# An RWKV layer with a routed mixture of experts on one core: other opening and closing steps, and expert slots spread over three more places

## The chip, the cores and the metric

The kernel runs on one core of one Trainium2 chip, as one program. The metric is the device time of one execution in microseconds. Before the change it is 512.9 us, the median of three runs (509.98, 512.90, 513.15). The profile is of one further execution.

## What is computed

8192 tokens (32 sequences of 256) of 128 channels, all in float32. Each token is normalised, goes through an RWKV block (time mixing with the WKV recurrence, then channel mixing) and, beside it, through a mixture of 8 experts (one shared expert for all, one routed expert for each token). The two results are multiplied, and the input is added:

```python
xn = _layernorm(x)
# s: the RWKV block of xn
h = _ln(xn); hx = _shift(h)
k, v, sr = (h*tmk + hx*(1-tmk)) @ att_kw.T, (h*tmv + hx*(1-tmv)) @ att_vw.T, sigmoid((h*tmr + hx*(1-tmr)) @ att_rw.T)
x2 = xn + (sr * _wkv(time_decay, time_first, k, v)) @ att_ow.T
h = _ln(x2); hx = _shift(h)
kk = square(relu((h*f_tmk + hx*(1-f_tmk)) @ f_kw.T))
s = x2 + sigmoid((h*f_tmr + hx*(1-f_tmr)) @ f_rw.T) * (kk @ f_vw.T)
# m: shared expert plus the one routed expert of the largest logit, both silu(x@wg.T)*(x@wu.T)@wd.T
m = swiglu(xn, shared) + swiglu(xn * sigmoid(max logit), expert[argmax logit])
out = x + silu(m) * s
```

## The kernel before, in words

**Tiling.** A tile is 128 tokens, a chunk is 512 tokens (two sequences, four tiles); there are 16 chunks, c = 0 to 15. PENULT is chunk 14 and LAST chunk 15. Every engine has its own program, written out by hand; semaphores tie them together. TensorE (PE) does matmuls and transposes, VectorE (DVE) scans and sums, ScalarE (ACT) activations and copies out of PSUM, GpSimd (POOL) small statistics, some 128x512 operations and the DMAs that it issues itself, SyncE (SP) all other DMAs.

**Opening.** For each chunk: x is loaded (L277), DVE takes statistics (`first_stats`, L1056) and combines them (`first_aggregate`, L1062), which it does for chunk c-1 after the statistics of chunk c. POOL makes the inverse deviation and the bias (L905 to L911), ACT normalises (`first_xn`, L625), PE transposes (L339) and ACT copies to the tile XT (`first_xt`, L631). Logits for the routing and the first parts of the shared expert are interleaved. Weights are loaded from ACT's queue (L619), eight DMAs before ACT's first activation. POOL's `second_rstd` (L915 to L921) gives what `make_z1` (L1129) needs.

**Steps.** From step i = 1 to 14 (`step(i)` of each engine) the WKV of chunk i, the channel mixing of chunk i-1 and its end for chunk i-2 run side by side. Eight places k = 0 to 7 in a step hold fill-in work, given by the table PLAN: parts of the shared expert and the routing in steps 1 to 5, then the expert slots. An expert slot n does, for one of 71 tiles of 128 sorted tokens, eight matmuls up (L473), two matmuls down of slot n-2 (L487), one transpose (L480), on ACT two or three activations (L737, L745, L728), on DVE one product (L1249) and on POOL a scatter of the rows to DRAM (L961). Slots 71 and 72 only finish those before them. Up to step 5, POOL also scatters the tokens to DRAM in expert order (L953). In the middle of all this SP copies x of chunks 0 to 11 to the output by one DMA from DRAM to DRAM (L300), once the first expert weights are on their way.

In each step ACT switches its table twice (L800 to the exp and log set, L810 back), and the work between is a chain through ACT and DVE.

**Closing** (`last_steps`). Chunks 14 and 15 finish. For both, x2 is made by DVE (L1199, with L1202 and L1206), its inverse deviation by POOL (`rstd_of_x2`, L935 to L941), z2 by ACT (L680), transposed by PE (`z2_transpose`, L398), turned to h2 (L689), mixed by DVE (`channel_mixes`, L1213 and L1216), and goes through the matmuls `ffn_receptance` (L405), `ffn_key` (L420) and `ffn_value` (L430). Meanwhile routed and shared output are added for all 16 chunks, in two ways: the odd chunks are loaded by SP (L313) into four buffers RR and added on PE by two matmuls with the identity (`final_sum`, L499 and L500); the even ones are added to XT by a DMA of POOL that accumulates (`final_add`, L975). ACT applies silu (L754, L758), DVE multiplies (`final_gate`, L1255). For chunks 0 to 11 a DMA of POOL adds the result to the copy of x in the output (`final_store`, L983); for chunks 12 to 15 DVE adds x (L1259) and SP stores (L317).

Of the kernel before, what the change touches and what calls it, by code (L numbers as in the profile page):

```python
# [7 lines left out]
P = 128  # L8
CHUNK = 512
# [23 lines left out]
NCST = K_TOK + TILES  # L33
# [3 lines left out]
ADDED = 12  # L37


def plan():  # L40
# [26 lines left out]
BY_PE = list(range(1, CHUNKS, 2))  # L67
BY_DMA = list(range(0, CHUNKS, 2))


def program(nc, x, vecs, cst, att_w, f_kw, f_vw, gate_w, sh_up, sh_dn, ex_w, out):
# [7 lines left out]
    with ctx:  # L79
# [71 lines left out]
        RR = [EW[u][:, 0:CHUNK] for u in range(4)]  # L151
# [8 lines left out]
        s_wa = sem("attention_and_shared_weights_loaded")  # L160
        s_fill = sem("xs_dram_filled")
# [41 lines left out]
        s_fx = [sem(f"final_x_loaded{u}") for u in range(4)]  # L203
        s_fr_in = [sem(f"final_routed_loaded{u}") for u in range(4)]
        s_fa = [sem(f"final_routed_added{u}") for u in range(4)]
        s_fy, s_fw, s_fv, s_fo = sem("final_y"), sem("final_silu"), sem("final_gated"), sem("final_out")
        s_pre, s_last = sem("x_copied_to_out"), sem("last_chunks_stored")
        s_out = [sem(f"out_stored{u}") for u in range(4)]
# [38 lines left out]

        RT_CHOSEN = 4
# [24 lines left out]
        def _(sp):  # L273
# [5 lines left out]
            for c in range(CHUNKS):  # L279
                load_x(c)  # L280
            sp.wait_ge(s_pad, 2)
# [18 lines left out]
            sp.dma_start(out[0:ADDED * CHUNK, :], x[0:ADDED * CHUNK, :]).then_inc(s_pre, 16)  # L300
            for c in range(5):
                sp.wait_ge(s_sct[c], 16 * TPC * (1 if c < 4 else CHUNKS - 4))
            for n in range(NEW + AHEAD):
                load_rows(n)
            for n in range(NEW, XTILES):
                load_weights(n)
                if n + AHEAD < XTILES:
                    load_rows(n + AHEAD)

            def load_final_routed(n):  # L310
                if n >= 4:
                    sp.wait_ge(s_fy, n - 3)
                sp.dma_start(tiles(RR[n % 4]), rows(routed_dram, BY_PE[n])).then_inc(s_fr_in[n % 4], 16)  # L313

            def store(c):
                sp.wait_ge(s_fo, c - ADDED + 1)
                sp.dma_start(rows(out, c), xn(c)).then_inc(s_last, 16)  # L317

            sp.wait_ge(s_xn, CHUNKS)
            for c in range(ADDED, CHUNKS):  # L320
                sp.dma_start(tiles(XI[c % 4][:, :]), rows(x, c)).then_inc(s_fx[c % 4], 16)
            for u in range(NXH):
                sp.wait_ge(s_yo[u], 16 * sum(1 for m in range(2, XTILES + 2) if m % NXH == u))
            for n in range(len(BY_PE)):
                load_final_routed(n)
            for c in range(ADDED, CHUNKS):
                store(c)
            for u in range(4):
                sp.wait_ge(s_out[u], 16 * (ADDED // 4))
            sp.wait_ge(s_last, 16 * (CHUNKS - ADDED))  # L330

        @block.tensor
        def _(pe):
# [67 lines left out]
            def ffn_receptance(c):  # L401
                pe.wait_ge(s_mix2, 2 * c + 1)
                b = BK if c == LAST else FB
                for j in range(TPC):
                    last = nc.tensor.matmul(part(b, j, CH), part(XR2, j, P), part(ATT, 4, CH), start=True, stop=True)  # L405
                last.then_inc(s_fr, 1)

            def ffn_key(c, q):
                if q == 0:
                    pe.wait_ge(s_mix2, 2 * c + 2)  # L410
# [3 lines left out]
                elif q == 1 and c == LAST:  # L414
                    pe.wait_ge(s_rk, 4 * c)
                elif q == 1:
# [3 lines left out]
                nc.tensor.matmul((FA, FB)[q % 2][:, :], part(FKW, q, P), XK2[:, :], start=True, stop=True)\  # L420
# [70 lines left out]
            def final_sum(n):  # L491
                b, c = RING[n % 3], BY_PE[n]
                pe.wait_ge(s_fr_in[n % 4], 16 * (n // 4 + 1))
# [5 lines left out]
                nc.tensor.matmul(b[:, :], ident, RR[n % 4], start=True, stop=False)  # L499
# [933 lines left out]
```

## Time and profile before

| what | value |
|---|---|
| median of the runs | 512.9 us |
| the profiled execution | 512.97 us |
| its span, first to last instruction | 511.2 us |
| busy: PE, DVE, ACT, POOL | 87%, 78%, 69%, 60% |

The span is 1.8 us shorter than the execution's own time, and all times below count from its start. An engine's busy time says how long its instructions ran, not whether anything waited for them; that is read from the timeline, where a row has its start, its length, the engine and line, what it writes and reads, and in brackets the idle time before it with what ended it.

### The profile page before, as it was taken

The numbers are of one execution on the slowest core, as the hardware profiler recorded it, in microseconds if no ns is written. First come the engines' busy times: TensorE is split into PE (matmuls) and PEld (weight loads), VectorE is DVE, ScalarE is ACT, GpSimd is POOL, SyncE is SP. The second block draws the span as 40 slices with busy tenths as digits, with TensorE's granted clock in tenths as the row PEclk, the third lists the DMA queues.
The fourth block names the chain that finished last, engine by engine and source line by source line (L and its number), as shares of the span: only waits on it lengthen the run. The fifth ranks groups of instructions, "written<-read, shape, count | busy, mean of one in ns | idle before, by whom it ended". The sixth has DMA issues, their size and how long they took to land. (4 is left out here: it accounts for less than half of the span.)

```text
span 511.2 us, 8965 instructions
## 1 busy us (share of the span) xinstructions
PE 446.2 (87%) x2655; PEld 332.9 (65%) x2655; DVE 397.5 (78%) x788; ACT 350.6 (69%) x706; POOL 307.5 (60%) x339
## 2 busy tenths in 40 slices
PE   0899897789899899899999999999999999977990
PEld 0567675356366465769696969686969696844650
DVE  4473959979669695979797979797979796987672
ACT  3768767375373746788787877778887887684860
POOL 6843686288677787228383838372828282846871
PEclk9999998599899999999999999999999999997996
DMA  8792000012911101226565556454656554427799
GB/s 270 224 275 60 2 0 1 5 48 88 378 50 48 44 32 49 54 79 168 164 167 163 173 157 177 153 160 131 173 159 177 155 171 147 124 82 121 107 189 161
DMA packets 62592, 64.97 MB, mean 127 GB/s; under 512 B 5776, under 2 KB 50705, under 8 KB 62496
## 3 DMA queue, kind: packets, MB, share of 16 engines
q1 hardware_dynamic: 46512, 49.06, 34.1%
q0 software_dynamic: 14880, 13.78, 13.0%
q10 hardware_dynamic: 1152, 1.56, 0.9%
q8 instruction: 22, 0.36, 0.3%
q14 instruction: 26, 0.21, 0.1%
HBM read 46.86 MB, written 21.12 MB: 133 GB/s over the span
## 5 line engine op out<-in xcount | busy, mean ns | idle before, releaser
L961 POOL DMA_INDIRECT routed_out<-xh,xs x71 | 94.1, 1326 | 46.5 <-ACT xh L745 30.0
L953 POOL DMA_INDIRECT tokens_by_expert<-xn,pos x64 | 66.8, 1044 | 27.8 <-issue 27.8
L473 PEld LDWEIGHTS bank_ring<-xh,ew 128*128 128x128 f32 x568 | 70.3, 192 | 10.6 <-issue 9.6
L473 PE MATMUL bank_ring<-xh,ew 128*128 128x128 f32 x568 | 75.4, 276 | 1.3 <-DVE hx L1249 0.8
L430 PE MATMUL bank_out<-fvw,kk 128*128 128x128 f32 x512 | 66.0, 275 | 0.0
L1224 DVE TENSOR_TENSOR kk<-rk 128x512 f32<-128x512 f32 x32 | 22.7, 711 | 53.3 <-ACT rk L703 49.8
L430 PEld LDWEIGHTS bank_out<-fvw,kk 128*128 128x128 f32 x512 | 61.9, 192 | 2.9 <-issue 2.9
L737 ACT ACTIVATE px<-bank_ring 128x256 f32<-128x256 f32 x71 | 27.0, 380 | 26.0 <-PE bank_ring L473 21.5
L487 PE MATMUL bank_ring<-ew,hx 128*128 128x128 f32 x284 | 43.5, 276 | 0.4 <-issue 0.4
L935 POOL TENSOR_SCALAR x_sm<-x_mv 128x4 f32<-128x4 f32 x16 | 4.4, 274 | 61.5 <-DVE x_mv L1206 60.7
L1241 DVE TENSOR_TENSOR hs<-tg,bank_ring 128x512 f32<-128x512 f32 x32 | 21.6, 676 | 24.6 <-ACT tg L721 11.0
L487 PEld LDWEIGHTS bank_ring<-ew,hx 128*128 128x128 f32 x284 | 37.8, 193 | 0.6 <-issue 0.6
L440 PEld LDWEIGHTS bank_ring<-sdn,hs 128*128 128x128 f32 x256 | 30.7, 192 | 11.3 <-DVE hs L1241 6.4
L451 PE MATMUL bank_ring<-xt,sup 128*128 128x512 f32 x64 | 35.9, 644 | 1.6 <-issue 1.6
L420 PE MATMUL bank_fb<-xk,fkw 128*128 128x512 f32 x64 | 33.7, 609 | 3.2 <-ACT tf L697 2.4
L457 PE MATMUL bank_ring<-xt,sup 128*128 128x512 f32 x64 | 35.5, 638 | 0.5 <-issue 0.3
L949 POOL TENSOR_TENSOR rw<-den_num,lq 128x512 f32<-128x512 f32 x16 | 22.2, 1387 | 21.5 <-issue 19.6
L745 ACT ACTIVATE xh<-bank_ring 128x256 f32<-128x256 f32 (+1 forms) x75 | 27.8, 370 | 8.2 <-PE bank_ring L487 5.6
L680 ACT ACTIVATE z<-x,x_sm 128x128 f32<-128x128 f32 x64 | 26.4, 483 | 10.2 <-POOL x_sm L941 10.2
L440 PE MATMUL bank_ring<-sdn,hs 128*128 128x128 f32 x256 | 31.6, 276 | 2.1 <-DVE hs L1241 2.1
L420 PE MATMUL bank_fa<-xk,fkw 128*128 128x512 f32 x64 | 32.9, 596 | 0.0
L1249 DVE TENSOR_TENSOR hx<-px,bank_ring 128x256 f32<-128x256 f32 x71 | 29.1, 409 | 0.5 <-ACT px L737 0.5
(167 smaller groups left out, 1116.8 us busy)
## 6 DMA issues: line engine op xcount, KB each, us to landing
ew<-ex_w SPq DMA_DIRECT2D x71, 384.0 KB
tokens_by_expert<-pad_row SPq DMA_DIRECT2D x1, 4686.0 KB, 21.4
xs<-tokens_by_expert SPq DMA_DIRECT2D x71, 66.0 KB
xi<-x SPq DMA_DIRECT2D x12, 256.0 KB, 4.5
out<-xn POOLq DMA_DIRECT2D x12, 256.0 KB, 8.2
ew<-routed_out SPq DMA_DIRECT2D x8, 256.0 KB, 4.2
xt<-routed_out POOLq DMA_DIRECT2D x8, 256.0 KB, 6.3
routed_out<-xh,xs POOLq DMA_INDIRECT x71
```

Source lines behind the costliest of these rows:

```text
L420: nc.tensor.matmul((FA, FB)[q % 2][:, :], part(FKW, q, P), XK2[:, :], start=True, stop=True)\
L430: last = nc.tensor.matmul(part(BO, j, CH), KK[:, q * CHUNK + j * P:q * CHUNK + (j + 1) * P], part(FVW, q, CH), start=(q + j == 0), stop=(q ...
L440: last = nc.tensor.matmul(part(b, j, CH), h[:, q * CHUNK + j * P:q * CHUNK + (j + 1) * P], part(SDN, q, CH), start=(q == 0), stop=(q == EQ ...
L451: nc.tensor.matmul(ring(5 * m + 3 * q)[:, :], part(SUP, q, P), part(XT, m, CHUNK), start=True, stop=True)\
L457: nc.tensor.matmul(ring(5 * m + 3 * q + 1)[:, :], part(SUP, EQ + q, P), part(XT, m, CHUNK), start=True, stop=True).then_inc(s_su, 1)
L473: last = nc.tensor.matmul(part(GU[n % 2], q, P), part(w, q, P), xt[:, 0:P], start=True, stop=True)
L487: last = nc.tensor.matmul(BX[:, P:P + CH], part(h, q, P), part(w, 2 * EQ + q, CH), start=(q == 0), stop=(q == EQ - 1))
L737: nc.scalar.activation(PX[n % 2][:, :], GU[n % 2][:, 0:EF], ACT.Silu).then_inc(s_px, 1)
L745: nc.scalar.activation(XH[n % NXH][:, a:b], BX[:, a:b], ACT.Copy).then_inc(s_xh, 1)
L953: nc.gpsimd.indirect_dma_start(xs_dram, bass.IndirectOffsetOnAxis(ap=POS[:, t:t + 1], axis=0), XN[:, t * XROW:(t + 1) * XROW], None).then_ ...
L961: nc.gpsimd.indirect_dma_start(routed_dram, bass.IndirectOffsetOnAxis(ap=XS[(n - 2) % NXS][:, CH:CH + 1].bitcast(i32), axis=0), XH[n % NXH ...
L1249: nc.vector.tensor_tensor(HX[n % NHX][:, :], PX[n % 2][:, :], GU[n % 2][:, EF:2 * EF], ALU.mult)\
```

## The change

1. **Opening.** DVE combines the statistics of chunks 0 to 3 right after taking them. ACT loads its second table only after the third chunk. `token_numbers` of POOL moves from behind the first chunk to behind chunk 3. The two channel-mixing weights (FKW, FVW) are loaded by SP after x of chunk 11, not by ACT at the start.
2. **No copy of x to the output.** Instead x of chunks 0 to 9 is loaded by SP between the loads of the expert slots (one after every fifth) into ten buffers, chunks 10 to 15 when a buffer is free again.
3. **Expert slots** are spread over 78 places in place of 75: places 0 to 2 of the last step are added.
4. **Closing.** POOL issues no DMAs any more. SP loads the routed output of all 16 chunks into ten buffers. Nine chunks are added by POOL with a 128x512 addition, seven on PE. x is added by POOL for chunks 0 to 14, by DVE for 15, and SP stores all chunks. The inverse deviation of x2 for chunks 14 and 15 is made by ACT (`Ln`, then `Exp`), the bias still by POOL. The product rw of chunk 15 moves from POOL to DVE. x2 of chunk 14 moves behind the WKV of chunk 15. The mixes of chunk 15 have tiles of their own (E1, E2), and the order of the last step is another on each engine.

```diff
     places = [(E_STEP, k) for k in range(5, 8)] + [(i, k) for i in range(E_STEP + 1, CHUNKS - 1) for k in range(8)]
+    places += [(CHUNKS - 1, k) for k in range(3)]
...
-BY_PE = list(range(1, CHUNKS, 2))
-BY_DMA = list(range(0, CHUNKS, 2))
+BY_PE = [1, 3, 5, 7, 9, 11, 13]
+BY_POOL = [c for c in range(CHUNKS) if c not in BY_PE]
+NRR, NXB = 10, 10
...
-            sp.dma_start(out[0:ADDED * CHUNK, :], x[0:ADDED * CHUNK, :]).then_inc(s_pre, 16)
...
+            def load_final_x(c):
...
+                elif c >= NXB:
+                    sp.wait_ge(s_fo, c - NXB + 1)
+                sp.dma_start(tiles(XB[c % NXB]), rows(x, c)).then_inc(s_fx0 if c < NXB else s_fx[c - NXB], 16)
...
+                if n % 5 == 0 and 3 <= n // 5 < 3 + NXB:
+                    load_final_x(n // 5 - 3)
...
+            for c in range(CHUNKS):
+                load_final_routed(c)
+            for c in range(CHUNKS):
                 store(c)
+                if c + NXB < CHUNKS:
+                    load_final_x(c + NXB)
...
@@ scalar
-            nc.scalar.preload_act_table_set("silu_and_others")
             for c in range(CHUNKS):
                 first_xn(c)
+                if c == 2:
+                    nc.scalar.preload_act_table_set("silu_and_others")
...
+            def rstd_of_x2(c):
+                act.wait_ge(s_mv2, TPC * (c + 1))
...
+                nc.scalar.activation(SM2[:, 0:TPC], stats(MV2, 0, TPC)[1], ACT.Ln, bias=CST[:, K_EPS:K_EPS + 1])\
+                  .then_inc(s_sm2, 1)
...
+                nc.scalar.activation(SM2[:, TPC:2 * TPC], SM2[:, 0:TPC], ACT.Exp, scale=-0.5).then_inc(s_rs2, 1)
...
                 nc.scalar.preload_act_table_set("natural_log_exp_and_others")
+                inverse_of_den(LAST)
+                rstd_of_x2(PENULT)
                 make_z2(PENULT)
-                inverse_of_den(LAST)
                 make_h2(PENULT)
+                rstd_of_x2(LAST)
+                make_z2(LAST)
                 nc.scalar.preload_act_table_set("silu_and_others")
+                make_h2(LAST)
...
@@ gpsimd
+            def final_sum(n):
+                c = BY_POOL[n]
+                y = part(XT, c, CHUNK)
...
+                nc.gpsimd.tensor_tensor(y, RR[c % NRR], y, ALU.add).then_inc(s_fp, 1)
+
+            def final_out(c):
                 pool.wait_ge(s_fv, c + 1)
...
+                nc.gpsimd.tensor_tensor(xn(c), xn(c), tiles(XB[c % NXB]), ALU.add).then_inc(s_fo, 1)
...
@@ vector
+            def make_rw(c):
...
+                nc.vector.tensor_tensor(RW[:, :], NUM, LQ[:, :], ALU.mult).then_inc(s_rw, 1)
...
                 first_stats(c)
-                if c > 0:
+                if c < 4:
+                    first_aggregate(c)
+                elif c > 4:
                     first_aggregate(c - 1)
```

The order of work at the places that matter most. DVE at the very start of the opening, before the change (bs holds partial statistics, mv the combined ones):

```order
L1056 BN_STATS bs<-xi 128x6 x8
L1062 BN_AGGR mv<-bs 128x2 x4
L1354 TENSOR_SCALAR vectors<-vectors 128x1
L1056 BN_STATS bs<-xi 128x6 x4
L1062 BN_AGGR mv<-bs 128x2 x4
```

and with the change:

```order
L1126 BN_STATS bs<-xi 128x6 x4
L1132 BN_AGGR mv<-bs 128x2 x4
L1126 BN_STATS bs<-xi 128x6 x4
L1132 BN_AGGR mv<-bs 128x2 x4
L1445 TENSOR_SCALAR vectors<-vectors 128x1
```

The first chunk's statistics are now combined before those of the second are taken.

DVE in the last step, from the mixes of chunk 14 on, before the change (x_1 is x2 of chunk 15, d and then xr, xk the mixes, kk the squares, xn<-xt,xn the final products):

```order
L1213 TENSOR_TENSOR d<-h 128x512
L1216 SCALAR_TENSOR_TENSOR xr<-d,vectors,h 128x512
L1216 SCALAR_TENSOR_TENSOR xk<-d,vectors,h 128x512
L1199 TENSOR_TENSOR x_1<-bank_k,xn 128x512
L1202 BN_STATS x_bs<-x_1 128x6 x4
L1206 BN_AGGR x_mv<-x_bs 128x2 x4
L1224 TENSOR_TENSOR kk<-rk 128x512 x2
L1255 TENSOR_TENSOR xn<-xt,xn 128x4x128 x2
L1213 TENSOR_TENSOR d<-h 128x512
L1216 SCALAR_TENSOR_TENSOR xr<-d,vectors,h 128x512
L1216 SCALAR_TENSOR_TENSOR xk<-d,vectors,h 128x512
```

and with the change:

```order
L1269 TENSOR_TENSOR x_1<-bank_k,xn 128x512
L1272 BN_STATS x_bs<-x_1 128x6 x4
L1276 BN_AGGR x_mv<-x_bs 128x2 x4
L1287 TENSOR_TENSOR d<-h 128x512
L1290 SCALAR_TENSOR_TENSOR xr<-d,vectors,h 128x512
L1290 SCALAR_TENSOR_TENSOR xk<-d,vectors,h 128x512
L1298 TENSOR_TENSOR kk<-rk 128x512
L1287 TENSOR_TENSOR d<-h 128x512
L1290 SCALAR_TENSOR_TENSOR e<-d,vectors,h 128x512 x2
L1298 TENSOR_TENSOR kk<-rk 128x512
L1329 TENSOR_TENSOR xn<-xt,xn 128x4x128 x2
```

The mixes of chunk 14 now stand behind x2 of chunk 15, and the mixes of chunk 15 between the two squares of chunk 14.

POOL in the last step, before the change (xt holds shared plus routed output, xn the product, x_sm the small statistics of x2):

```order
L975 DMA xt<-routed_out 128x4x128 x3
L949 TENSOR_TENSOR rw<-den_num,lq 128x512
L975 DMA xt<-routed_out 128x4x128
L935 TENSOR_SCALAR x_sm<-x_mv 128x4
L936 TENSOR_SCALAR x_sm<-x_mv 128x4
L938 TENSOR_TENSOR x_sm<-x_sm,minus_half 128x4
L941 TENSOR_TENSOR x_sm<-x_sm 128x4
L975 DMA xt<-routed_out 128x4x128 x4
L983 DMA out<-xn 128x4x128 x12
```

and with the change, up to the first of the additions of x (ew, d, xv and z are buffers of the routed output):

```order
L1005 DMA routed_out<-xh,xs 8192x128 x2
L1026 TENSOR_TENSOR xt<-ew,xt 128x512 x2
L1014 TENSOR_SCALAR x_sm<-x_mv 128x4
L1018 TENSOR_TENSOR x_sm<-x_sm 128x4
L1026 TENSOR_TENSOR xt<-ew,xt 128x512
L1014 TENSOR_SCALAR x_sm<-x_mv 128x4
L1018 TENSOR_TENSOR x_sm<-x_sm 128x4
L1026 TENSOR_TENSOR xt<-d,xt 128x512
L1026 TENSOR_TENSOR xt<-xv,xt 128x512
L1026 TENSOR_TENSOR xt<-ew,xt 128x512 x3
L1026 TENSOR_TENSOR xt<-z,xt 128x512
L1034 TENSOR_TENSOR xn<-xn,xi 128x4x128 x4
```

Twenty DMAs are gone from POOL, and 24 operations of 128x512 stand in their place (9 of L1026, 15 of L1034).

## Rows read from the trace of the kernel before

**Rows 1.** Page: granted clock of TensorE, tenths, in 40 equal slices.

```profile
PEclk9999998599899999999999999999999999997996
```

**Rows 2.** Timeline of the opening: start us, length us, engine, line, what, [idle before].

```profile
6.51 0.37 DVE L1062 BATCH_NORM_AGGREGATE mv<-bs 128x2 f32<-128x6 f32 x4
...
9.06 0.87 DVE L1056 BATCH_NORM_STATS2 bs<-xi 128x6 f32<-128x128 f32 x4 [2.15 <-DMA xi<-x]
9.12 1.65 ACT L625 ACTIVATE xn<-xi,nb,rs 128x128 f32<-128x128 f32 x4 [1.35 <-POOL nb L911]
...
12.34 1.65 ACT L625 ACTIVATE xn<-xi,nb,rs 128x128 f32<-128x128 f32 x4 [1.57 <-POOL nb L911]
...
14.57 1.64 ACT L625 ACTIVATE xn<-xi,nb,rs 128x128 f32<-128x128 f32 x4
...
17.56 0.69 DVE L1129 TENSOR_TENSOR z<-xn,r 128x512 f32<-128x512 f32 x1 [4.04 <-POOL r L921]
```

**Rows 3.** Timeline around SP's copy of x, and one row of step 4.

```profile
128.96 0.66 SPq L300 DMA_DIRECT2D out<-x  x1
...
133.66 0.60 ACT L697 ACTIVATE tf<-bank_fb 128x512 f32<-128x512 f32 x1 [3.69 <-remote]
...
134.31 1.75 PE L420 MATMUL bank_fb<-xk,fkw 128*128 128x512 f32 x2 [2.45 <-ACT tf L697]
...
135.85 1.91 PE L365 MATMUL bank_k<-xk,att 128*128 128x512 f32 x2
...
191.02 0.60 ACT L697 ACTIVATE tf<-bank_fb 128x512 f32<-128x512 f32 x1 [2.25 <-remote]
```

**Rows 4.** ACT's table loads at L800, in steps 9 and 10.

```profile
323.44 1.28 ACT L800 ACT_TABLE_LOAD   x1
...
348.59 1.28 ACT L800 ACT_TABLE_LOAD   x1
```

**Rows 5.** Windows: length, busy us of each engine, granted clock, DMA share, GB/s.

```profile
374.07:399.55 25.48, 24.50 (x176) 20.64 (x175) 22.03 (x40) 20.35 (x46) 14.48 (x14) 1.00 0.57 168
425.76:448.23 22.47, 20.94 (x141) 16.90 (x140) 19.72 (x35) 17.09 (x34) 13.20 (x14) 1.00 0.38 110
...
490.00:500.00 10.00, 8.45 (x42) 5.39 (x40) 9.34 (x15) 5.01 (x10) 9.04 (x7) 1.00 1.40 201
```

**Rows 6.** POOL's d1 between two scans of DVE, and such a scan alone.

```profile
52.47 2.06 POOL L927 TENSOR_TENSOR d<-h 128x512 f32<-128x512 f32 x1 [4.75 <-ACT h L646]
52.47 1.22 DVE L1164 TENSOR_TENSOR_SCAN bb_aa<-e 128x514 f32<-128x514 f32 x1
...
53.61 2.00 DVE L1168 TENSOR_TENSOR_SCAN bb_aa<-e,ev 128x514 f32<-128x514 f32 x1
...
118.68 1.23 DVE L1168 TENSOR_TENSOR_SCAN bb_aa<-e,ev 128x514 f32<-128x514 f32 x1
```

**Rows 7.** All d1 of POOL, nearest to its new additions.

```profile
L927 POOL TENSOR_TENSOR d<-h x16: 1034/1040/2057, 26.7 to 436.9; 128x512 f32<-128x512 f32 x16
```

**Rows 8.** Timeline of the closing.

```profile
463.62 1.11 PE L398 MATMUL bank_fb<-consts,z 128*128 128x128 f32 x4 [5.79 <-ACT z L680]
...
471.37 0.69 DVE L1199 TENSOR_TENSOR x<-bank_k,xn 128x512 f32<-128x512 f32 x1 [2.23 <-PE bank_k L389]
...
482.70 1.02 PE L420 MATMUL bank_fa<-xk,fkw 128*128 128x512 f32 x2
...
489.68 4.91 DVE L1255 TENSOR_TENSOR xn<-xt,xn 128x512 f32<-128x512 f32 x8 [0.31 <-ACT xt L754]
...
497.39 1.05 PE L430 MATMUL bank_out<-fvw,kk 128*128 128x128 f32 x8
...
500.73 0.69 DVE L1259 TENSOR_TENSOR xn<-xn,xi 128x512 f32<-128x512 f32 x1
```

**Rows 9.** Landing times of SP's loads L313.

```profile
DMA to landing us min/median/max: 3.0/4.2/5.9
```

**Rows 10.** Landing times of SP's stores L317.

```profile
DMA to landing us min/median/max: 5.2/7.4/8.4
```

More of the change, by code:

```diff
@@ L402, in ffn_receptance @@
                 pe.wait_ge(s_mix2, 2 * c + 1)
-                b = BK if c == LAST else FB
+                b = {PENULT: BK, LAST: BV}.get(c, FB)
+                if c == PENULT:
+                    pe.wait_ge(s_x2, CHUNKS)
                 for j in range(TPC):
-                    last = nc.tensor.matmul(part(b, j, CH), part(XR2, j, P), part(ATT, 4, CH), start=True, stop=True)
+                    last = nc.tensor.matmul(part(b, j, CH), part(mixed2(c)[0], j, P), part(ATT, 4, CH), start=True, stop=True)
                 last.then_inc(s_fr, 1)
@@ L419, in ffn_key @@
                     pe.wait_ge(s_rk, 4 * c + q - 1)
-                nc.tensor.matmul((FA, FB)[q % 2][:, :], part(FKW, q, P), XK2[:, :], start=True, stop=True)\
+                nc.tensor.matmul((FA, FB)[q % 2][:, :], part(FKW, q, P), mixed2(c)[1][:, :], start=True, stop=True)\
                   .then_inc(s_fk, 1)
@@ L498, in final_sum @@
                     pe.wait_ge(s_xh, XTILES + 4)
[L499 removed]
+                nc.tensor.matmul(b[:, :], ident, RR[c % NRR], start=True, stop=False)
                 nc.tensor.matmul(b[:, :], ident, part(XT, c, CHUNK), start=False, stop=True).then_inc(s_fy, 1)
@@ L555, in last_steps @@
                 attention_out(PENULT)
-                for q in range(FQ):
-                    ffn_value(PENULT - 1, q)
-                    if q < FQ - 1:
-                        fill(LAST, q + 1)
-                z2_transpose(PENULT)
+                ffn_value(PENULT - 1, 0)
+                fill(LAST, 1)
+                ffn_value(PENULT - 1, 1)
+                fill(LAST, 2)
+                ffn_value(PENULT - 1, 2)
+                fill(LAST, 3)
+                ffn_value(PENULT - 1, 3)
                 final_sum(0)
@@ L843, in last_steps @@
                 ffn_square(LAST, 2)
-                final_silu(5)
-                final_silu(6)
-                for c in range(7, CHUNKS):
+                for c in range(6, CHUNKS):
                     final_silu(c)
@@ L1019, in last_steps @@
             def last_steps():
[L1020 to L1031 removed]
+                fill(LAST, 0)
+                fill(LAST, 1)
+                fill(LAST, 2)
+                fill(LAST, 3)
+                final_sum(0)
+                final_sum(1)
+                negative_mean_of_x2(PENULT)
+                final_sum(2)
+                negative_mean_of_x2(LAST)
+                final_sum(3)
+                final_sum(4)
+                final_sum(5)
+                final_sum(6)
+                final_sum(7)
+                final_sum(8)
+                final_out(0)
+                final_out(1)
+                final_out(2)
+                final_out(3)
+                final_out(4)
+                final_out(5)
+                final_out(6)
+                final_out(7)
+                final_out(8)
+                final_out(9)
+                final_out(10)
+                final_out(11)
+                final_out(12)
+                final_out(13)
+                final_out(14)
             first(0)
[L1034 removed]
             for c in range(1, CHUNKS):
                 first(c)
+                if c == 3:
+                    token_numbers()
                 if c == 2:
@@ L1335, in last_steps @@
                 final_gate(4)
+                final_gate(5)
                 ffn_square(LAST, 3)
-                for c in range(5, LAST):
-                    final_gate(c)
+                final_gate(6)
+                final_gate(7)
+                final_gate(8)
+                final_gate(9)
+                final_gate(10)
+                final_gate(11)
+                final_gate(12)
+                final_gate(13)
+                final_gate(14)
                 make_s(LAST)
```

175 lines of the change are left out of this document (94 added, 81 removed).

## The prediction

> **What bounds the kernel now.** I read the slices of the page first, then the windows by stage, then the timeline of three places (opening, around the copy of x, closing), and last the chain that ended last. In the slices the reader is to see where TensorE falls from its full clock of 2.4 GHz: around slices 6 to 10 and at slice 36 [rows 1]; a clock of 0.5 is its lower level of 1.2 GHz. In the expert steps a whole step takes 25.48 us with PE busy 24.50 and DVE 22.03 [rows 5]: PE sets the pace, DVE is close behind. The opening is a chain DVE, POOL, ACT, PE that x and the order of DVE hold back [rows 2]. In the closing PE waits 5.79 us for z2 of chunk 14 [rows 8], the DMA engines are more than full (share 1.40) [rows 5], and DVE's last sum ends at 501.42 [rows 8], 9.8 us before the span ends at 511.2: the last store takes that long behind POOL's accumulating DMAs. So three stages have something to give, and each is taken by itself. The sum is made against the profiled execution, 512.97 us (span 511.2 and 1.8 around it), which is 0.1 above the median of the runs, 512.9.
>
> **Opening: -2.0 us.** The first statistics are combined at 6.51, after those of chunk 1; they are ready at 4.9, 1.6 earlier. Chunk 1 is combined behind the wait for x of chunk 2 (9.06) and now at 6.6; POOL needs 2.24 us from the end of a combination (6.88) to xn (9.12) [rows 2]. Chunk 2: 9.06 + 0.87 + 0.37 + 2.24 = 12.5 in place of 14.57. The product z, on which PE's first transpose for the WKV waits, comes behind that, 2.0 earlier than 17.56, and the stage behind it is a chain through all engines, so it keeps this. The weights taken off the start (512 KB) can only bring x of chunk 2 sooner. Bounds: -1.0 (the chunk behind is held by its own x) and -3.0 (x comes 1 us sooner). The table load moved behind chunk 2 was beside the wait for POOL before and costs 1.28 us [rows 4] at most if ACT is late there; this lies within the bounds.
>
> **Copy of x: -3.0 us.** SP starts it at 128.96. From then ACT does nothing for 3.69 us though its matmul is done; PE waits 2.45 us for it, and then runs at half clock: 1.75 and 1.91 us for pairs that take 1.02 [rows 3, 8]. The trace puts this wait down to nothing on the core ("remote"); I take it for something that ACT fetches through the DMA engines, held up by the copy. Cost: 2.45 + 0.73 + 0.89 = 4.1. In step 4, with no copy, ACT waits 2.25 in the same way [rows 3], so part stays. Bounds -1.0 and -4.1; I take -3.0, nearer to the row with the copy since PE there had slack for the shorter wait. The ten loads of x in the expert steps add 2.5 MB at a DMA share of 0.57 [rows 5]: nothing. Without that cover, each would hold an expert's weights up by about 1 us, with five slots loaded ahead.
>
> **Expert slots: +1.2 us.** By the table, steps 6 to 13 now have four places without a slot, before one; step 14 has eight full slots, before five and two that are only remainders. Step 14 took 22.47 us, a full step 25.48 [rows 5]: +3.0. What does an empty place save? Step 10 has one, and from its neighbour's table load at 323.44 to its own at 348.59 it took 25.15 [rows 4]: 0.33 less, where PE's own work of a slot is 1.3 (the two windows differ by 35 instructions and 3.56 us of PE, and a slot has 13), because DVE's chain is then late. The new empty places stand behind the WKV, where the next product is not behind the wide sums: I take 0.6 each. So -4 x 0.6 + 0.33 + 3.0 = +0.9, and 0.3 for slot 72, which stands behind ACT's table load in the last step. Bounds: -2.0 (1.3 each) and +2.5 (0.33 each and slot 72 in full).
>
> **Closing: +2.0 us,** in two parts. Times are those of the trace before, without the shifts above.
>
> First, PE's chain. Scatters of slots 71 and 72 end at about 459.5, SP sees them 1.1 later, the routed rows of chunk 1 land 3.0 after their issue [rows 9] and 1 behind chunk 0: PE starts its sums at about 464.5, again at half clock after its wait, as it did at 463.62 [rows 8]. x2 of chunk 15 thus comes at 471.4 as before [rows 8]. But the mixes of chunk 14 now stand behind it: 471.4 + 2.3 (sum and statistics) + 3 x 0.69 + one of POOL's additions between them = 476.6. ACT makes z2 of chunk 15 by 476.4, loads a table (1.28 [rows 4]), makes h2 and two relus: 480.1. DVE's square, difference and first mix of chunk 15, with two of POOL's additions between them, end at 483.3. PE's receptance and three values (0.9 each) end at 487.0, where the first key of chunk 15 began at 482.70 [rows 8]: +4.3. From there PE took 15.74 us to its last matmul at 498.44; now one final sum (1.7) less: 501.0. DVE's last four operations need 2.98 [rows 8]: 504.0.
>
> Second, DVE against POOL. POOL's d1 and DVE's scans, all reading two SBUF tiles, do not run together: d1 takes 2.06 in place of 1.04 behind one scan, and the next scan, 1.23 alone, takes 2.00 behind d1 [rows 6, 7]. The scans end 1.92 apart, where back to back they would end 1.15 apart. So one POOL operation between two of DVE costs 0.8 us. DVE's final products take 0.61 each back to back [rows 8]. From the end of PE's values of chunk 14 and DVE's first sum after them (487.9) there stand 19 such DVE operations and 13 additions of POOL: 19 x 0.61 + 13 x 0.8 = 22.0, so 509.9. That is later than PE's 504.0 and decides. The last store lands 3.0 to 3.2 after its issue, as the least loaded loads do [rows 9], since no DMA of POOL is left: 513.1, against 511.2. Bounds: 0.69 per POOL operation (its end to the scan's end, without overlap) gives 0.6; 1.04, its whole length [rows 7], gives 5.1; a store at 5.2 [rows 10] adds 2. Below: nothing of it binds, the first rival.
>
> The Trainium skill says in "SBUF — State Buffer", section "Who interferes with whom", that a VectorE instruction with two SBUF inputs contends with a GpSimd one that reads SBUF, and that the first holds the port for its whole instruction. That it blocks, rows 6 show; the whole length would be 1.04 + 0.08 for each POOL operation, and is the third case below.
>
> Sum: 512.97 - 2.0 - 3.0 + 1.2 + 2.0 = 511.2; I say **511.0**.
>
> **Rivals.** (a) *The port does not bind* (0.27). POOL's additions slip into DVE's waits, and PE's chain sets the end: 504.0, less 1.6 for the POOL operations counted in it, and 3.1 for the store: 505.5, 5.7 under before. 512.97 - 2.0 - 3.0 + 1.2 - 5.7 = 503.5. For it: DVE idles in places of the closing until 489. Against: its final products come in one burst of 4.91 us for eight [rows 8], just when POOL's additions of x are due. (b) *Early gains are used up later* (0.13): POOL's scatters or the pad of the expert rows hold the steps, so opening and copy give nothing: 511.2 + 5.0 = 516. Against: SP's loads of expert rows find PE still in other work. (c) *Each operation holds the port whole* (0.15): place, the last 20 us and the sums before; price 1.12 in place of 0.8 for each of 21 POOL operations that meet DVE, 0.32 x 21 = 6.7; time 518, slower than before. It decides from about 1.05 per operation on.
>
> **Numbers.** The forecast has 0.45, its own range is 506 to 517. A measurement of this kernel can tell about 1% (5.1 us) from no change. Faster by over 1% (under 507.8): all of (a) and a fifth of the forecast, 0.37. Slower by over 1% (over 518.0): half of (c), a part of (b) and of the forecast's upper end, 0.17. The same: 0.46. The range to (a) and (c): 502.5 to 518.
>
> **What would show it.** Opening: z made at about 15.5. Copy: no idle ACT of 3.7 us near 130 and no half clock there. Slots: steps 6 to 13 shorter by 2 us in all, step 14 at 25.5. Closing: POOL's additions of x with a median near 1.7 in place of 1.04, DVE's final products near 1.4, one ready for each of POOL's; DVE's last sum about 8 us after PE's last matmul in place of 3; the last store lands within 4 us. The forecast is wrong if the final products stay at 0.7 (then a), or if PE is idle for over 6 us in the last step.

## The result, and the profile after

| what | before | after |
|---|---|---|
| median of the runs on the same chip | 511.45 us | 523.61 us |
| the profiled execution | 512.97 us | 522.44 us |
| its span | 511.2 us | 520.6 us |

The change makes the kernel slower: ratio 1.023, 95% interval 1.017 to 1.029, which is 9 to 15 us; whether it is more than 2% stays open. Forecast were 511.0 us and a range of 502.5 to 518. The time lies above it, and the third rival (518, each POOL operation holds DVE for its whole length) is the nearest. The ratios leave out runs in a slow state of the chip, among them one of the four after (530.45 us, which is in the median) and the profiled execution of weights_one_by_one in experiment 6 (532.12 us).

In after the lines have moved: the table load of L800 is L841, POOL's additions are L1026 (routed output) and L1034 (x), DVE's final products L1329, its last sum L1333. Where the time went is read from the table load to the exp and log set, of which both kernels have one in each step. From one such load to another (us, one profiled execution of each kernel):

| stage | before | after | difference |
|---|---|---|---|
| start to the load of step 1 | 105.88 | 104.08 | -1.8 |
| to the load of step 5 | 115.37 | 115.71 | +0.3 |
| to the load of step 13 | 204.51 | 203.06 | -1.4 |
| to the load of step 14 | 22.47 | 24.88 | +2.4 |
| from there to the end | 62.97 | 72.87 | +9.9 |

Timeline of the opening of after (start us, length us, engine, line, what, [idle before]), which answers to [rows 2]:

```profile
6.71 0.38 DVE L1132 BATCH_NORM_AGGREGATE mv<-bs 128x2 f32<-128x6 f32 x4
7.58 1.65 ACT L659 ACTIVATE xn<-xi,nb,rs 128x128 f32<-128x128 f32 x4 [1.49 <-POOL nb L955]
9.56 1.65 ACT L659 ACTIVATE xn<-xi,nb,rs 128x128 f32<-128x128 f32 x4 [0.34 <-POOL nb L955]
...
12.61 1.65 ACT L659 ACTIVATE xn<-xi,nb,rs 128x128 f32<-128x128 f32 x4 [0.72 <-POOL nb L955]
...
15.80 0.69 DVE L1199 TENSOR_TENSOR z<-xn,r 128x512 f32<-128x512 f32 x1 [3.28 <-POOL r L965]
```

z is made 1.76 us sooner (forecast: 2.0), and in this pair of profiles the first stage keeps it.

Timeline of after around the place where the copy stood, ACT and PE, which answers to [rows 3]:

```profile
131.87 0.60 ACT L739 ACTIVATE tf<-bank_fb 128x512 f32<-128x512 f32 x1 [3.66 <-remote]
...
132.52 2.08 PE L453 MATMUL bank_fb<-xk,fkw 128*128 128x512 f32 x2 [2.45 <-issue]
...
137.56 0.60 ACT L745 ACTIVATE rk<-bank_fb 128x512 f32<-128x512 f32 x1 [2.25 <-remote]
```

There is no copy, and ACT stops for 3.66 us in place of 3.69, PE for 2.45 as before, and then PE runs at half clock (granted clock 0.50 from 133 to 135). Step 2, in which this lies, takes 34.1 us after and 32.7 before. The copy was beside the stop and not its cause. The trace of before shows a stop of the same length once more, in a row that the prediction overlooked. It is ACT's, 36 us behind the start of the copy (DMA share 0.16 from 140 to 160):

```profile
165.09 0.60 ACT L715 ACTIVATE xt<-bank_ring 128x512 f32<-128x512 f32 x1 [3.68 <-remote]
```

Windows of after, the first cut as the second of [rows 5], the rest from the table load of step 14 on (from:to, length, busy us of PE, its weight loads, DVE, ACT, POOL, granted clock, DMA share, GB/s):

```profile
422.85:447.73 24.88, 23.90 (x173) 20.28 (x172) 20.89 (x39) 19.19 (x42) 14.98 (x14) 1.00 0.39 117
447.73:464.00 16.27, 9.30 (x57) 6.85 (x55) 13.49 (x25) 11.88 (x19) 5.12 (x4) 0.98 0.10 26
464.00:480.00 16.00, 12.53 (x40) 6.40 (x40) 6.27 (x14) 6.68 (x14) 9.11 (x10) 0.81 0.94 238
480.00:500.00 20.00, 17.32 (x81) 11.19 (x82) 17.49 (x18) 14.21 (x27) 15.01 (x11) 1.00 0.46 129
500.00:520.60 20.60, 3.26 (x20) 2.32 (x18) 15.62 (x12) 1.66 (x4) 14.51 (x9) 0.69 0.52 156
```

The last row is the new tail: 20 us in which PE has almost nothing left, and DVE and POOL are both busy. Timeline of DVE and POOL there, which answers to [rows 8]:

```profile
482.06 1.76 DVE L1287 TENSOR_TENSOR d<-h 128x512 f32<-128x512 f32 x1
...
492.01 1.76 DVE L1298 TENSOR_TENSOR kk<-rk 128x512 f32<-128x512 f32 x1
...
497.65 14.07 DVE L1329 TENSOR_TENSOR xn<-xt,xn 128x512 f32<-128x512 f32 x9
...
501.32 1.95 PE L463 MATMUL bank_out<-fvw,kk 128*128 128x128 f32 x16
...
506.12 6.72 POOL L1034 TENSOR_TENSOR xn<-xn,xi 128x512 f32<-128x512 f32 x4
...
515.10 0.69 DVE L1333 TENSOR_TENSOR xn<-xn,hs 128x512 f32<-128x512 f32 x1
```

A final product takes 14.07 / 9 = 1.56 us on average; before, eight took 4.91 [rows 8], 0.61 each. DVE's and POOL's operations stand in strict alternation: four of POOL's in 6.72 us, 1.68 each, and a product of DVE for each of them. DVE's last sum ends 12.5 us after PE's last matmul (515.79 and 503.27); before it was 2.98.

The span ends 4.8 us behind DVE's last sum, but this is not all the store. What SP waited for from 500 on (us in total, times, longest):

```profile
SPq L81 <- PEq L81: 2.3, 1, 2.3
SPq L81 <- DMA out<-xn: 1.9, 1, 1.9
```

L81 is where the program closes and the engines meet. The last store is waited for during 1.9 us, and then SP waits 2.3 us for PE, whose last matmul ended 17 us before the end of the span. In before that last wait is 1.0, in x_on_dve 0.2; why it differs was not looked into.

### The profile page after: what moved, and what is told of

Same layout as the page of the kernel before. It is cut to its first block, busy times and chain, and to the rows that moved or that the text cites. A ratio compares the mean times of both kernels' runs of the same rounds, so it can differ in the third digit from the quotient of the medians.

```text
span 520.6 us, 8992 instructions
## 1 busy us (share of the span) xinstructions
PE 443.4 (85%) x2651; PEld 332.4 (64%) x2651; DVE 411.5 (79%) x786; ACT 351.8 (68%) x710; POOL 312.2 (60%) x338
## 3 DMA queue, kind: packets, MB, share of 16 engines
q10 hardware_dynamic: 864, 1.04, 0.6%
## 4 chain that ended last, share of the span: by engine, by line
PE 28%; ACT 12%; issue 9%; DVE 9%; DMA 1%; POOL 0%; DVEq 0%; ACTq 0%; SPq 0%; POOLq 0%
PE bank_ring L506 9%; PE bank_ring L520 5%; PE bank_out L463 5%; ACT L841 2%; DVE xn L1329 2%; ACT rk L745 2%; ACT L851 2%; PE bank_fb L435 2%; PE bank_fa L453 2%; PE bank_fb L453 2%; PE bank_ring L513 2%; ACT lq L705 1%; DVE e L1221 1%; DVE e L1222 1%; ACT kk L753 1%
## 5 line engine op out<-in xcount | busy, mean ns | idle before, releaser
L1298 DVE TENSOR_TENSOR kk<-rk 128x512 f32<-128x512 f32 x32 | 26.7, 833 | 52.3 <-ACT rk L745 50.0
L463 PE MATMUL bank_out<-fvw,kk 128*128 128x128 f32 x512 | 66.3, 275 | 0.0
L1315 DVE TENSOR_TENSOR hs<-tg,bank_ring 128x512 f32<-128x512 f32 x32 | 21.6, 674 | 23.1 <-ACT tg L763 10.8
L484 PE MATMUL bank_ring<-xt,sup 128*128 128x512 f32 x64 | 35.8, 643 | 2.4 <-issue 2.4
L453 PE MATMUL bank_fb<-xk,fkw 128*128 128x512 f32 x60 | 32.0, 616 | 4.3 <-issue 3.9
L490 PE MATMUL bank_ring<-xt,sup 128*128 128x512 f32 x64 | 34.5, 622 | 0.3 <-issue 0.3
L993 POOL TENSOR_TENSOR rw<-den_num,lq 128x512 f32<-128x512 f32 x15 | 19.3, 1290 | 21.3 <-issue 21.2
L453 PE MATMUL bank_fa<-xk,fkw 128*128 128x512 f32 x60 | 30.9, 596 | 1.0 <-ACT rk L745 1.0
```

The costliest lines, as they stand in the source:

```text
L453: nc.tensor.matmul((FA, FB)[q % 2][:, :], part(FKW, q, P), mixed2(c)[1][:, :], start=True, stop=True)\
L463: last = nc.tensor.matmul(part(BO, j, CH), KK[:, q * CHUNK + j * P:q * CHUNK + (j + 1) * P], part(FVW, q, CH), start=(q + j == 0), stop=(q ...
L484: nc.tensor.matmul(ring(5 * m + 3 * q)[:, :], part(SUP, q, P), part(XT, m, CHUNK), start=True, stop=True)\
L490: nc.tensor.matmul(ring(5 * m + 3 * q + 1)[:, :], part(SUP, EQ + q, P), part(XT, m, CHUNK), start=True, stop=True).then_inc(s_su, 1)
```

## The experiments

Each is compared with the kernel before on the same chip; line numbers in their profiles are shifted by a few. The kernel after stands at 1.023.

**1. x_left_out: is it POOL's additions of x?**

```diff
             def last_steps():
...
-                final_out(0)
...
-                final_out(14)
```

> The kernel after without POOL's 15 additions of x (its output lacks x in chunks 0 to 14). Theory P (each POOL addition costs the DVE operation beside it 1.06 us): the nine final products that took 14.07 us take 5.5, the two squares of chunk 15 0.7 each in place of 1.76, so PE's last matmul is over at about 501.5 and DVE at 504.5; 523 becomes 511 to 512, ratio to the kernel before 0.995 to 1.005. Rival C (PE's own later chain and the landing of loads and stores set the end, the products only fill the wait for it): DVE waits between its products, and the time stays above 519.

Measured: ratio 1.001 (0.9975 to 1.005), 2.2 points or 11 us less than after, for 15 additions. Groups of the last step of after and then of this kernel (busy us, mean ns of one, idle before):

```profile
L1329 DVE TENSOR_TENSOR xn<-xt,xn 128x512 f32<-128x512 f32 x16 | 20.6, 1337 | 0.1
```

```profile
L1306 DVE TENSOR_TENSOR xn<-xt,xn 128x512 f32<-128x512 f32 x16 | 10.2, 686 | 2.1 <-ACT xt L796 1.5 <-ACT xt L799 0.5
```

The products have lost half their time and now wait for ACT, 2.1 us in all: something else, PE's chain, sets the end again. DVE's last sum ends 3.0 us behind PE's last matmul. Rival C falls. One thing expected didn't come: PE's last matmul is no earlier. It ends 56.3 us after the table load of step 14; in after it is 55.5 and in before 50.2. PE ran its values of chunk 14 at about half clock here (granted clock 0.58 and 0.56 from 488 to 492, and 1.00 in after). So even without these additions PE's chain in the new order is 6 us longer than before, and that eats the 7 us by which the span now ends sooner behind DVE's last sum (2.9 in place of 9.8).

**2. x_on_dve: the same additions on DVE.**

```diff
-                nc.gpsimd.tensor_tensor(xn(c), xn(c), tiles(XB[c % NXB]), ALU.add).then_inc(s_fo, 1)
+                nc.vector.tensor_tensor(xn(c), xn(c), tiles(XB[c % NXB]), ALU.add).then_inc(s_fo, 1)
```

> The kernel after with the 15 additions of x on DVE, each behind the next product, in place of POOL. Theory P: 15 x 0.62 us more work for DVE, but all at 0.62 each; from 486.7 its work is 23.5 us, so it ends at about 510, 5.6 sooner than 515.8; time 517, ratio 1.01. Rival R (a 128x512 operation on POOL relieves DVE, and DVE's slow products have another cause, such as their own operands): the products stay at 1.56 us and the additions come on top, time 530 or more.

Measured: ratio 1.0075 (1.003 to 1.012), 516.45 us. DVE does 15 operations more and is done sooner. Timeline of its DVE near the end, products L1306 and additions L1318 by turns:

```profile
503.39 0.68 DVE L1318 TENSOR_TENSOR xn<-xn,tg 128x512 f32<-128x512 f32 x1
504.00 0.68 DVE L1306 TENSOR_TENSOR xn<-xt,xn 128x512 f32<-128x512 f32 x1
504.60 0.68 DVE L1318 TENSOR_TENSOR xn<-xn,xi 128x512 f32<-128x512 f32 x1
```

They start 0.60 us apart. So one addition costs DVE 0.60 us when it does it itself, and 1.08 (1.68 - 0.60, from the profile of after) when POOL does it. The time is within a microsecond of the 517 expected. Its parts are less close: DVE's last sum ends at 512.1 where 510 was expected, and the span ends 2.8 us behind it.

**3. sums_early: POOL's additions of routed output.** From experiment 2, with two of them moved ahead.

```diff
                 final_sum(2)
-                negative_mean_of_x2(LAST)
                 final_sum(3)
                 final_sum(4)
+                negative_mean_of_x2(LAST)
```

> The kernel x_on_dve with two of POOL's additions of routed output moved ahead of its small statistics of x2 of chunk 15. Theory P (those additions hold the mixes of chunk 15, 1.76 us for a difference that takes 0.69): the difference and the two mixes of chunk 15 take 2.1 us in place of 4.1, PE's idle 2.17 us before the receptance of chunk 15 goes, all behind it is 2 us earlier; ratio 1.003 in place of 1.0075. Rival U (the mixes wait for ACT's h2 and PE for the values anyway): nothing moves, ratio 1.007 or more.

Measured: ratio 1.0004 (0.9975 to 1.003), 0.7 points less than experiment 2. Timeline of its DVE at the mixes of chunk 15, and PE's receptance behind them:

```profile
484.73 0.68 DVE L1264 TENSOR_TENSOR d<-h 128x512 f32<-128x512 f32 x1
485.45 1.41 DVE L1267 SCALAR_TENSOR_TENSOR e<-d,vectors,h 128x512 f32<-128x512 f32 x2
...
486.25 1.16 PE L435 MATMUL bank_v<-att,e 128*128 128x128 f32 x8 [0.20 <-DVE e L1267]
```

The difference takes 0.68 in place of 1.76, the two mixes 1.41 in place of 2.31, and PE waits 0.20 in place of 2.17. So POOL's additions also made PE's own chain later, where the prediction had counted two of them at 0.8 each. Of the 0.7 points, 3.6 us, the profiles show less: from the table load of step 14 to the end it is 64.9 us in place of 66.3.

**4. x_half: what one meeting costs.**

```diff
-                nc.gpsimd.tensor_tensor(xn(c), xn(c), tiles(XB[c % NXB]), ALU.add).then_inc(s_fo, 1)
+                nc.gpsimd.tensor_tensor(xn(c)[:, 0:2, :], xn(c)[:, 0:2, :], tiles(XB[c % NXB])[:, 0:2, :], ALU.add)\
+                  .then_inc(s_fo, 1)
```

> The kernel after with POOL's additions of x on the first two of the four tiles of each chunk (its output lacks x in the other two). Theory P1 (a POOL operation holds DVE's for nearly its own length, 1.26 us less an overlap of 0.2): half the length, 0.65, costs 0.45, so a product behind it takes 1.05 to 1.1 us in place of 1.75 and one product and one addition alternate every 1.05 us. Rival P2 (a fixed cost of about 1.06 us for each change between the two engines, whatever the length): products stay at 1.6 us or more. Time by P1 515, ratio 1.003.

Measured: ratio 1.0055 (1.001 to 1.010). Timeline, nine products of DVE, four of POOL's additions beside them, and its last one, which goes ahead of DVE's and shows its own length:

```profile
496.70 9.48 DVE L1330 TENSOR_TENSOR xn<-xt,xn 128x512 f32<-128x512 f32 x9 [0.19 <-ACT xt L799]
...
502.20 4.57 POOL L1034 TENSOR_TENSOR xn<-xn,xi 128x256 f32<-128x256 f32 x4
...
506.73 0.72 POOL L1034 TENSOR_TENSOR xn<-xn,hs 128x256 f32<-128x256 f32 x1
```

One of each every 4.57 / 4 = 1.14 us, a little over the 1.05 to 1.1 expected. Less DVE's own 0.60 that is 0.54 for an addition that takes 0.72 alone; in after it is 1.68 - 0.60 = 1.08 for one that takes 1.27 alone (timeline of after, one beside which DVE is idle):

```profile
466.71 1.27 POOL L1026 TENSOR_TENSOR xt<-ew,xt 128x512 f32<-128x512 f32 x1 [1.03 <-DMA ew<-routed_out]
```

Both times the price is POOL's length less 0.18 or 0.19: it follows the length, and P2, a fixed price, falls. The time, 515.05 us, is the 515 expected.

**5. copy_later: the copy and the stop.** From the kernel before.

```diff
-            sp.dma_start(out[0:ADDED * CHUNK, :], x[0:ADDED * CHUNK, :]).then_inc(s_pre, 16)
             for c in range(5):
                 sp.wait_ge(s_sct[c], 16 * TPC * (1 if c < 4 else CHUNKS - 4))
+            sp.dma_start(out[0:ADDED * CHUNK, :], x[0:ADDED * CHUNK, :]).then_inc(s_pre, 16)
```

> The kernel before with SP's copy of x moved from 129 us to behind the scatters (near 205 us). Theory of the prediction (the copy holds ACT, PE and DVE for 3.7 us near 130): that stop falls below 1.5 us, time 2 to 3 us less, ratio 0.995. Rival S (the stop is there without a copy, as in the kernel after with 3.66 us): ACT's idle time stays at 3.7 us, and the time within 1 us, ratio 1.000.

Measured: ratio 1.012 (1.004 to 1.020). Timeline of ACT, and of SP:

```profile
136.95 0.60 ACT L697 ACTIVATE tf<-bank_fb 128x512 f32<-128x512 f32 x1 [3.67 <-remote]
...
209.01 0.65 SPq L302 DMA_DIRECT2D out<-x  x1
209.72 7.15 SPq L289 DMA_DIRECT2D xs<-tokens_by_expert  x9
...
220.92 0.99 ACT L728 ACTIVATE xs<-xs 128x128 f32<-128x128 f32 x3 [5.82 <-DMA xs<-tokens_by_expert]
```

The stop is 3.67 us without the copy beside it: rival S is right about the stop. Its time, within 1 us of before, was missed, since neither theory had counted the new place. The rows of the first slots are loaded right behind the copy, ACT waits 5.82 us for them, and step 5 (table load to table load) takes 33.7 us in place of 25.3. So a copy of 3 MB, of which no cost is seen at 129 us, costs 6 (by the ratio, whose interval is 2 to 10) to 8 us (by step 5) at 209. That the rows stand behind it there is what this wait points to; it was not tried apart.

**6. weights_one_by_one and weights_after_scatters: is it the five expert weights?** From the kernel after; in the first each load stands behind the scatters of one of the first chunks, in the second all five behind all scatters:

```diff
-            for n in range(NEW):
-                load_weights(n)
             for c in range(5):
                 sp.wait_ge(s_sct[c], 16 * TPC * (1 if c < 4 else CHUNKS - 4))
+            for n in range(NEW):
+                load_weights(n)
```

> The kernel after with SP's first five loads of expert weights (384 KB each, issued from 121.8 to 127.1 us in a row) put each behind the scatters of one of the first chunks. Theory W (the burst of five loads is what holds PE's releases): ACT's idle time of 3.66 us near 131 falls below 1.5, that of 2.25 near 137 too, and the half clock there goes; time 2 to 3 us less than 523. Rival S2 (the stop belongs to this place of PE's program, whatever the DMA queues carry): it stays at 3.7 us, time within 1 us of 523.

> The kernel after with SP's first five loads of expert weights behind all scatters (near 204 us), so that nothing but POOL's scatters uses DMA from 122 to 200 us. Theory W (the burst of five loads makes the stop near 131): ACT's idle of 3.66 us there falls below 1.5, and step 2 (table load to table load, 34.1 us) to 30 or 31. Rival S2 (it is in PE's program or made by the scatters): it stays at 3.7 us, and step 2 at 34. In either case step 5 gets longer by the time that the first slots wait for weights, 3 to 6 us, so the whole time is 523 to 529.

Measured: ratios 1.015 (1.007 to 1.023), which can't be told from after, and 1.040 (1.034 to 1.045), 533 us and so beyond the 523 to 529 expected. Timeline of ACT in the second, which has nothing but POOL's scatters on the DMA engines there:

```profile
127.85 0.60 ACT L739 ACTIVATE tf<-bank_fb 128x512 f32<-128x512 f32 x1 [0.34 <-PE bank_fb L435]
...
139.19 0.60 ACT L745 ACTIVATE rk<-bank_fa 128x512 f32<-128x512 f32 x1 [3.26 <-remote]
...
170.34 0.60 ACT L757 ACTIVATE xt<-bank_ring 128x512 f32<-128x512 f32 x1 [6.56 <-remote]
195.42 0.60 ACT L739 ACTIVATE tf<-bank_fb 128x512 f32<-128x512 f32 x1 [2.26 <-remote]
```

In the first the stop shrank to 1.58 us. In the second the stop at 131 is gone, 0.34 in place of 3.66, and step 2 takes 28.4 us in place of 34.1. But stops of the same kind, ACT waiting for PE whose matmuls ended long before by the trace, now stand at 139 and 170, step 3 takes 39.2 in place of 26.2, and step 5, whose first slots wait for loads that SP now issues late, 32.5 in place of 24.9. So W is right for the place and wrong for the gain, and S2 is wrong. What these stops are was not settled: they move when the loads move, they don't go, and the traffic of loads is not needed for them.

**7. opening_only.** The kernel before with part 1 of the change.

```diff
                 first_stats(c)
-                if c > 0:
+                if c < 4:
+                    first_aggregate(c)
+                elif c > 4:
                     first_aggregate(c - 1)
...
-            nc.scalar.preload_act_table_set("silu_and_others")
             for c in range(CHUNKS):
                 first_xn(c)
+                if c == 2:
+                    nc.scalar.preload_act_table_set("silu_and_others")
...
```

> The kernel before with the change's opening alone (statistics of chunks 0 to 3 combined at once, ACT's second table after chunk 2, token numbers after chunk 3, channel weights by SP). As predicted: z of chunk 0 is made near 15.8 in place of 17.56, and the stage behind keeps 1.8 to 2.0 us; ratio 0.996. Rival G (the steps up to 5 wait for something else, such as POOL's scatters): the first table load of step 1 comes 1.8 sooner, that of step 5 not; ratio 1.000.

Measured: ratio 0.9954 (0.992 to 0.999), -2.4 us. In this profile z of chunk 0 is made at 14.78, but the load of step 5 stands at 221.86, and in before at 221.25, so by itself the profile would speak for rival G. The steps up to 5 differ between single executions (the load of step 1 at 104.08 in after and at 107.46 in x_left_out, whose code is the same up to there). The claim therefore rests on the ratio, and so does not say in which stage the gain is kept; the -1.8 of the first table is not proof of it either.

**8. before_new_places and after_old_places: the slots.** The one line of the table, added to before and taken from after.

```diff
+    places += [(CHUNKS - 1, k) for k in range(3)]
```

> The kernel before with the change's table of slots alone (78 places). As predicted: steps 6 to 13 shorter by 1.4 to 2 us together, step 14 at 24.9 in place of 22.5, slot 72 in the last step 0.3: +0.9 to +1.2 us, ratio 1.002. Rival (the saving in the steps is PE's own work of 1.3 us for each of the four places): ratio 0.998 or less.

> The kernel after with the old table of slots (75 places, none in the last step). From the trace of after: steps 6 to 13 longer by 1.4 us, step 14 shorter by 2.4, and the last scatter, and with it PE's first final sum, 1.2 us sooner after the last step's table load: 2.2 us less than after, ratio near 1.019. Rival (as in before_new_places, where the same table cost 0.8%): 3.5 to 4 us less, ratio 1.015.

Measured: 1.008 (1.005 to 1.011), +4.1 us, and 1.009 (1.005 to 1.013), 7 us less than after, its profiled execution 3.3 less. Both are more than forecast, and the second is more than its rival too (1.015). In before_new_places steps 6 to 13 are 1.3 us shorter and step 14 is 2.4 longer, as expected, and what comes behind the table load of step 14 is 3.0 longer. In after_old_places this last part is 3.4 shorter than in after. Timeline of before_new_places there:

```profile
461.87 1.01 POOL L962 DMA_INDIRECT routed_out<-xh,xs  x1 [5.39 <-ACT xh L746]
463.18 1.88 POOL L962 DMA_INDIRECT routed_out<-xh,xs  x1 [0.30 <-issue]
465.13 0.95 POOL L936 TENSOR_SCALAR x_sm<-x_mv 128x4 f32<-128x4 f32 x1
...
471.10 1.11 PE L399 MATMUL bank_fb<-consts,z 128*128 128x128 f32 x4 [6.64 <-ACT z L681]
472.01 1.92 PE L500 MATMUL bank_ring<-ew,consts 128*128 128x512 f32 x2
```

The scatters of the last two slots now start 9.5 us after the table load at 452.40, since POOL waits for slot 72, and its small statistics of x2, the loads of routed output and with them PE's transpose and first sum stand behind them: the transpose starts 18.7 us after the table load in place of 15.4 [rows 5, 8].

**9. opening_and_8_by_dma and opening_and_10_by_dma: a version that keeps what gained.** The kernel before with the new opening, and DVE instead of POOL's DMA adds x for four (or two) chunks more.

```diff
-ADDED = 12
+ADDED = 8
...
+        FX = [t[:, :] for t in XI[0:4]] + [t[:, q * CHUNK:(q + 1) * CHUNK] for t in HS for q in range(EQ)]
...
-                    dve.wait_ge(s_fx[c % 4], 16)
-                    nc.vector.tensor_tensor(xn(c), xn(c), tiles(XI[c % 4][:, :]), ALU.add).then_inc(s_fo, 1)
+                    dve.wait_ge(s_fx[c % 8], 16)
+                    nc.vector.tensor_tensor(xn(c), xn(c), tiles(FX[c % 8]), ALU.add).then_inc(s_fo, 1)
```

> The kernel before with the change's opening, and with x added by DVE, not by POOL's accumulating DMA, for chunks 8 to 11 as well (12 of 16 chunks by DMA become 8). Theory Q (the last store takes 9.8 us because it stands behind POOL's accumulating DMAs): it lands within 5 us, DVE's last sum is 0.5 to 2 us later for four additions of 0.61, so the closing is 3 to 4 us shorter; with the opening ratio 0.988 to 0.991. Rival T (DVE is full there): DVE ends 2.5 us later and the store is still over 7 us: ratio 0.996 or more.

> The kernel opening_and_8_by_dma with x added by POOL's accumulating DMA for 10 chunks in place of 8. Theory Q: DVE has two additions less (1.2 us) of the 5.3 us between PE's last matmul and its own last sum, and the last store still lands within 5 us: ratio 0.985 to 0.988. Rival Q2 (with 10 the stores stand behind POOL's DMAs again): landing over 6 us, ratio 0.990 or more.

Measured: 0.988 (0.983 to 0.993) and 0.992 (0.9885 to 0.996); both are about 1% faster than before, and so faster than after. The intervals overlap, so which of 8 and 10 is better stays open. End of the first one's timeline:

```profile
495.71 1.05 PE L439 MATMUL bank_out<-fvw,kk 128*128 128x128 f32 x8
...
501.35 0.69 DVE L1269 TENSOR_TENSOR xn<-xn,hs 128x512 f32<-128x512 f32 x1
```

DVE ends at 502.04 and the span at 504.8: 2.8 us in place of 9.8. The closing (from the load of step 14, 447.66) takes 57.1 us in place of 63.0. The second one's last sum:

```profile
499.33 0.69 DVE L1269 TENSOR_TENSOR xn<-xn,hs 128x512 f32<-128x512 f32 x1
```

Its span ends at 506.2, 6.2 us behind this: what rival Q2 had said (over 6 us, ratio 0.990 or more), and theory Q (within 5 us, 0.985 to 0.988) is wrong for ten. Nor is DVE's last sum sooner with two additions less: 54.3 us after the table load of step 14 (445.74), and 54.4 with eight. With 8, 10 and 12 accumulating DMAs of POOL the span ends 2.8, 6.2 and 9.8 us behind DVE's last sum, which bears out that the last store stands behind them; with none at all, in x_on_dve, it is 2.8 too, so eight cost nothing there.

## Why the prediction was wrong, point by point

- **What bounds the kernel**: the stages and what holds them were read rightly, but for the stop at 130.
- **Opening, -2.0**: right in size, -2.4 by the ratio of experiment 7 and -1.8 in the trace of after; that the stage behind keeps it is not shown.
- **Copy of x, -3.0**: wrong. The step that failed is "I take it for something that ACT fetches through the DMA engines, held up by the copy". It was a cause read from a coincidence in time. The bound from step 4 (-1.0, where the same wait stood without a copy) was the sign not followed: two stops of one kind, one with and one without the copy. A third, at 165.09, had even the full 3.68 us. Measured 0: the stop is 3.66 us without any copy. What makes it stays open.
- **Expert slots, +1.2**: the steps came out near the forecast (6 to 13 shorter by 2, measured 1.4; step 14 +3.0, measured +2.4), but in part by luck. An empty place was put at 0.6; steps 7, 9, 11 and 13 of after, which have one each, take 25.32, 25.50, 25.16 and 25.16 us, and full ones 25.48, so it saves 0.3 at most. The rest of the 1.4 comes from steps 9 and 13 of before, which took 25.76 and 26.21 though they were full. The term that was mis-sized is "0.3 for slot 72": the last part got 3.0 us longer in before_new_places and 3.4 shorter in after_old_places. The whole is 3.3 to 4.1 by profiles and by the ratio on before, and 7 by the ratio against after, over the upper bound of 2.5. Counted was the work of the slot on PE; not counted was who waits for its scatter, the last one before all final sums.
- **Closing, +2.0**: the mechanism was right, DVE against POOL and not PE decides, and the size was off. The price was put at 0.8 per operation, from a pair of d1 and a scan [rows 6], and measured 1.08. The row in which POOL's operation stands alone, 1.04 [rows 7], was of another operation; the addition takes 1.27. So 13 meetings cost 13 x 0.28 = 3.6 us more than forecast: from DVE's first sum behind PE's values of chunk 14 to its last it took 25.7 us, and 22.0 were forecast. That stretch also began later: its first sum ended 42.4 us after the table load of step 14, and the forecast's 487.9 is 39.7 after it [rows 5]. Of these 2.7 us, 1.4 stood already when x2 of chunk 15 was made (24.6 in place of 23.1), behind the routed output that comes late with slot 72; the other 1.3 came up to the values, and at the mixes of chunk 15 the same price fell on DVE and through it on PE (experiment 3). The rival (c) had put the limit at "about 1.05 per operation", and it was passed.
- **The last store**: forecast were 3.0 to 3.2 after its issue. The store was waited for during 1.9 us only, but the span ends 4.8 after DVE's last sum, 1.6 more than forecast, because SP waits 2.3 us more for PE.
- **The sum of the closing**: its own +1.9 (rounded to 2.0), 2.7 for the later start, 3.7 for the price and 1.6 at the end give the +9.9 of the trace. That PE's chain without POOL's additions of x would be only 2.6 us longer than before (501.0 against 498.44) was wrong as well, but hidden here, since DVE ended later: in x_left_out it is 6 us longer.
- Experiments 1 to 3 fit this: with no addition of x on POOL and two sums moved, the kernel stands at 1.0004 (0.9975 to 1.003); the opening (-0.5%) and the slots (+0.8%) alone would make 1.003. So the rest of the closing, with an end that comes 7 us sooner behind DVE's last sum, gains little or nothing.
- The Trainium skill's rule in "SBUF — State Buffer", section "SBUF: two separate sides", by which whichever of the two starts first gets the shared pair of ports for its whole instruction, was made a rival with 0.15. (The section "Who interferes with whom", which the prediction names for it, calls the pair an exclusive lock, and speaks of the whole instruction for VectorE's two-port modes.) Worked out from the rule and the lengths alone, as an estimate, a meeting would cost 1.27 and 0.72; the trace shows 1.08 and 0.54. For the full length it is nearer than the 0.8 that was taken from one pair.

## What to carry to other kernels

In these kernels a GpSimd addition that runs while VectorE has a queue of operations on SBUF gives nothing: it costs VectorE more (1.08 us) than doing it itself (0.60 us), and moves all that waits for VectorE. Where VectorE waits for others such help may still be worth having; no run here tried that. Where it waits is read from the timeline row by row, not from busy shares. A wait that stands beside a transfer is not yet caused by it: look first for the same wait elsewhere in the trace (3.68 us at 165.09). And a piece of work put where an engine idles must be followed to who waits for its last result: slot 72 was counted with 0.3 us of work, and the last part of the kernel got 3 us longer.

## What was not expected of the hardware

- Where both engines have a queue, they alternate strictly, one operation each, at both lengths tried, and each pair takes the sum of the two less 0.18 or 0.19 us (1.68 for 0.60 and 1.27, 1.14 for 0.60 and 0.72).
- In the steps with scatters, ACT waits up to 6.6 us for matmuls that by the trace ended before; the stop near 131 keeps its length to 0.03 us between kernels (3.69, 3.66, 3.67), has a twin of 3.68 at 165 in before, and jumps to other places when SP's first five loads move. Its cause is open.
- The same copy of 3 MB costs nothing that the traces show at 129 us, and 6 to 8 us at 209, by its place alone.
- Behind a burst of POOL's accumulating DMAs the end of the last store depends on their number: 2.8, 6.2 and 9.8 us from DVE's last sum to the end of the span for 8, 10 and 12, and 2.8 for none.
